# A post-norm block of windowed attention and hashed experts: a new order behind the last scores, short spare products in TensorE's waits, and narrow products in the tile loop

## The chip, the core and the metric

The kernel runs on one core of a Trainium2 chip. The core's engines run side by side and meet at semaphores: TensorE multiplies (PE in the profile, its weight loads are PEld), VectorE (DVE) and ScalarE (ACT) work on what it leaves in PSUM, GpSimd (POOL) works in SBUF and issues indirect DMAs, SyncE (SP) issues the other DMAs. The metric is the device time of one execution in microseconds, as the median of several runs.

## What is computed

The reference takes x (4 x 512 x 128, float32), adds an attention to it, normalises, adds an expert layer, and normalises again:

```python
Q, K, V = heads(x @ wq), heads(x @ wk), heads(x @ wv)           # 16 heads of 8
local = _local_window_attn(Q, K, V)                             # blocks of 32, each sees itself and the one before
GK, GV = pool(x @ wgk), pool(x @ wgv)                           # means over 8 tokens: 64 latents, 8 heads of 8
rem = softmax(mask(GQ @ GK.T / sqrt(8))) @ GV                   # causal over the latents
out = sigmoid(Q . gate_l) * local + sigmoid(Q . gate_r) * (rem @ r_out_w)
x = layernorm(x + out @ w_out)
h = mod(int(x[:, 0] + x[:, 1]), 8)                              # the token's experts: h and h + 1
y = sum over e in {h, h+1}: 0.5 * (relu(x @ W1[e] + b1[e]) @ W2[e] + b2[e])
x = layernorm(x + y)
```

## The kernel before

The 2048 tokens are 16 tiles of 128 (T = 16), four to a batch row (KT_ = 4, NB = 4). Each engine has one instruction stream, written out by hand; nothing but this order and the semaphores sets when things run.

**The tile loop** (`for t in range(T + 3)` on every engine) is a pipeline three tiles deep. In iteration t TensorE makes the scores of tile t (`score_latent`, `score_rows`), subtracts the maxima that VectorE found (`largest`, `take_off`), ScalarE takes the exponentials (`exp`), TensorE transposes them one iteration later (`turn`, line 1244), ScalarE copies them to SBUF (PTs), and TensorE multiplies with the values: `weigh(t, 0)` and `weigh(t, 1)` for the 16 windowed heads (line 1259, the transposed probabilities as weights in pieces of 32 columns), and `weigh(t, 2)` for the latent heads (line 1266, k + 1 products with all 128 columns as weights, k being the tile's place in its batch row). `normalise` (VectorE) divides by the row sums, TensorE transposes `rem` (line 1361), multiplies with r_out_w (line 1377), `gate` adds the two parts to `att`, TensorE transposes `att` (line 1340) and multiplies with w_out (line 1347), and `residual` (VectorE) adds the input, writes y and takes its moments (lines 856 to 860). GpSimd and, for the last tile, VectorE (line 1011) finish the layer norm into x1. Once per batch row `fill(("G", b))` makes the latent keys and values (lines 1148 and 1151).

**Routing.** `mark` (VectorE) finds the expert of each token of a batch row, `fill(("R", ...))` and `rank_last` count ranks with products on TensorE, `place` turns ranks into rows of a buffer `groups` in HBM, and GpSimd scatters the rows there.

**Full tiles.** Behind the 12th tile's routing some expert groups already hold full tiles of 128 tokens. `full_tiles` and `full_rows` (VectorE, lines 923 to 944) work out for FULL = 5 such tiles the expert and the first row, and write them as integers to `full_table`. SyncE reads each entry into a register (`load_table`, line 306) and issues the loads: w1f (2 x 256 KB of W1, in WR = 3 buffers, line 354) and xrow (the tokens, line 364). `columns(j)` transposes a tile on TensorE (line 1286), `up_full` makes the two up products (lines 1295 and 1299), ScalarE does the relus, `down_full` the down products (line 1310). VectorE also reads the five expert numbers into registers (line 1017), since its `full_sum` picks the bias by them; then come `moments` and `finish`.

**Other tiles.** The remaining tiles are looped over at run time (`Fori`, lines 1417 to 1436 on TensorE), 17 of them here: 16 up passes, 16 down passes and a transpose each. VectorE does half of the second relus (line 1073), copies the next columns (line 1047), and finishes the tile before (`finish`, line 1041), for which it waits until the stores before that one have landed; GpSimd issues one indirect store per tile (lines 579 and 568).

**Clock.** At the start TensorE runs products of a constant tile `spare` (line 1317) while it waits for the first data.

What stands behind the last scores (t = 16, 17, 18) is the part that the change reorders:

- VectorE, t = 16: normalise(14), full_tiles, full_rows, residual(13), full_biases, gate(14); t = 17: normalise(15), residual(14), gate(15); t = 18: residual(15). Then line 1011, mark(3), place(3), count_tiles, and the five register loads.
- TensorE, t = 16: transposes and weighing of tile 15, line 1361 (which waits for residual(13), `summed`), 1377; t = 17: lines 1340, 1347, 1361, columns(0), 1377; t = 18: up_full(0, 0), line 1340, up_full(0, 1), line 1347.
- SyncE: the five xrow loads stand ahead of w1f of the second tile, and each w1f load waits until the one before has landed.

## Time and profile before

| | us |
|---|---|
| median of 3 runs (lowest to highest) | 242.28 (241.79 to 242.59) |
| the profiled execution, its own time | 243.42 |
| its span, from the first instruction to the last | 241.4 |
| PE busy in the span | 216.1 |
| DVE, ACT, POOL busy | 151.5, 121.5, 117.3 |

The profile is of one execution. Its span leaves 2.0 us outside, and its own time lies 1.14 us above the median of the runs. "Busy" of TensorE counts pipelined products with their latency, so a high share doesn't say that the array is full. A timeline row is: start, length, engine, line, operation, output and inputs, count, and in brackets the engine's idle time before it and what ended it. PEclk and the granted clock are TensorE's clock as a share of 2.4 GHz.

### The profile page before, as it was taken

How to read it: one execution, taken by the hardware profiler on the slowest of the kernel's cores; microseconds unless marked ns; L12 is line 12 of the kernel's file. 1: busy time of each engine (PE TensorE's matmuls, PEld its weight loads, DVE VectorE, ACT ScalarE, POOL GpSimd, SP SyncE). 2: the span in 40 equal slices, each digit the busy share in tenths (PEclk: the TensorE clock that was granted, in tenths of full speed). 3: DMA queues.
4: the chain of work that ended last, by engine and by line, in shares of the span. 5: the costliest groups of instructions: out<-in, count | busy, mean ns of one | idle time of the engine just before them, and what ended most of it. 6: DMA issues, size and time to landing. Idle time of an engine off the chain costs nothing.

```text
span 241.4 us, 9967 instructions
## 1 busy us (share of the span) xinstructions
PE 216.1 (90%) x3623; PEld 182.5 (76%) x3623; DVE 151.5 (63%) x523; ACT 121.5 (50%) x360; POOL 117.3 (49%) x218
## 2 busy tenths in 40 slices
PE   7979998999999999998996899897999999999930
PEld 3545777877888678886874599886899999999920
DVE  7835457795877867888898525374556656555640
ACT  3534656665577646765754246652434353434410
POOL 6453034661744428662747330648465465545541
PEclk9988999999999999999999569999999999999995
DMA  3231130032212233120001435412112112111100
GB/s 98 57 93 45 48 91 3 3 92 90 89 33 80 72 101 92 45 69 15 27 25 44 124 110 175 133 35 66 45 49 49 54 51 55 30 38 44 34 22 7
DMA packets 18553, 14.68 MB, mean 61 GB/s; under 512 B 2646, under 2 KB 15546, under 8 KB 18512
## 3 DMA queue, kind: packets, MB, share of 16 engines
q1 hardware_dynamic: 17008, 11.83, 17.5%
q0 software_dynamic: 1216, 2.16, 2.7%
q8 instruction: 27, 0.44, 0.8%
q10 hardware_dynamic: 288, 0.13, 0.2%
q14 instruction: 14, 0.11, 0.2%
HBM read 11.43 MB, written 3.03 MB: 60 GB/s over the span
## 4 chain that ended last, share of the span: by engine, by line
PE 64%; DVE 11%; issue 9%; DMA 6%; ACT 3%; POOL 2%; DVEq 2%; POOLq 1%; ACTq 0%
PE bS L1295 9%; PE bT L1244 7%; DMA out<-yo,idx 5%; PE bV L1435 4%; PE bV L1428 4%; PE bS L1187 4%; PE bV L1259 3%; PE bS L1212 3%; PE bV L1266 3%; PE bJ L1163 3%; PE bS L1226 2%; PE bL L1347 2%; PE bT L1295 2%; PE bS L1194 2%; PE bL L1361 2%
## 5 line engine op out<-in xcount | busy, mean ns | idle before, releaser
L681 ACT ACTIVATE ha<-bS,b1c 128x128 f32<-128x128 f32 x68 | 19.4, 368 | 40.0 <-PE bS L1295 40.0
L669 ACT COPY PTs<-bT 128x512 f32<-128x512 f32 (+3 forms) x48 | 25.8, 538 | 19.4 <-PE bT L1244 19.3
L568 POOL DMA_INDIRECT out<-yo,idx x18 | 19.2, 1067 | 17.8 <-POOL idx L564 9.8
L1244 PE MATMUL bT<-ident,Pr 128*128 128x128 f32 x168 | 27.4, 282 | 0.1
L1295 PE MATMUL bS<-xsT,w_s 128*128 128x128 f32 x204 | 26.4, 279 | 0.9 <-issue 0.8
L499 POOL TENSOR_SCALAR rstd<-mv 128x1 f32<-128x1 f32 x16 | 3.8, 235 | 45.7 <-DVE mv L860 45.7
L1295 PEld LDWEIGHTS bS<-xsT,w_s 128*128 128x128 f32 x204 | 24.1, 192 | 2.1 <-issue 2.1
L1244 PEld LDWEIGHTS bT<-ident,Pr 128*128 128x128 f32 x168 | 20.5, 147 | 4.1 <-issue 3.8
L515 POOL DMA_INDIRECT groups<-x,pos x16 | 16.6, 1035 | 12.5 <-DVE pos L910 9.1
L815 DVE TENSOR_REDUCE mx<-bS 128x8 bf16<-128x512 f32 x32 | 21.4, 676 | 0.0
L656 ACT ACTIVATE Pr<-bS 128x512 f32<-128x512 f32 x32 | 19.9, 622 | 2.6 <-PE bS L1226 2.6
L1435 PE MATMUL bV<-w_s,hb 128*128 128x128 f32 x136 | 19.0, 279 | 1.4 <-DVE hb L1073 1.4
L820 DVE TENSOR_REDUCE mx<-bS 128x8 bf16<-128x128 f32 (+3 forms) x16 | 7.8, 490 | 18.0 <-issue 10.6
L1435 PEld LDWEIGHTS bV<-w_s,hb 128*128 128x128 f32 x136 | 17.0, 191 | 2.0 <-DVE hb L1073 1.8
L1428 PE MATMUL bV<-w_s,ha 128*128 128x128 f32 x136 | 18.2, 276 | 0.3 <-DVE ysum L1023 0.2
L1073 DVE TENSOR_SCALAR hb<-bT,b1c 128x128 f32<-128x128 f32 x34 | 10.4, 346 | 11.7 <-PE bT L1295 9.2
L1428 PEld LDWEIGHTS bV<-w_s,ha 128*128 128x128 f32 x136 | 16.5, 192 | 0.7 <-ACT ha L681 0.7
L1259 PE MATMUL bV<-Vx,PTs 128*32 128x18 f32 x1024 | 15.2, 186 | 1.7 <-DVE rem L836 0.8
L1259 PEld LDWEIGHTS bV<-Vx,PTs 128*32 128x32 f32 x1024 | 12.3, 111 | 4.8 <-issue 3.4
L632 ACT COPY Vx<-bJ 64x256 f32<-64x256 f32 x32 | 12.0, 374 | 7.7 <-PE bJ L1163 7.5
L1041 DVE TENSOR_SCALAR yo<-y,mv,rstd 128x128 f32<-128x128 f32 x22 | 7.6, 344 | 9.8 <-DMA out<-yo,idx 5.8
L560 POOL TENSOR_TENSOR rstd<-rstd,half 128x1 f32<-128x1 f32 x22 | 12.7, 578 | 1.7
(236 smaller groups left out, 515.5 us busy)
## 6 DMA issues: line engine op xcount, KB each, us to landing
w_s<-in_L_ffn_W SPq DMA_DIRECT2D x16, 256.0 KB
w1f<-in_L_ffn_W SPq DMA_DIRECT2D x10, 256.0 KB, 2.7
xrow<-groups SPq DMA_DIRECT2D x22, 64.5 KB, 1.8
xs<-groups SPq DMA_DIRECT2D x18, 64.0 KB
x_tok<-in_L_attn_x SPq DMA_DIRECT2D x4, 256.0 KB, 3.2
groups<-padrows SPq DMA_DIRECT2D x1, 516.0 KB, 5.7
b2r<-in_L_ffn_b SPq DMA_DIRECT2D x1, 512.0 KB, 3.7
out<-yo,idx POOLq DMA_INDIRECT x18
```

The source lines that it names most:

```text
L515: nc.gpsimd.indirect_dma_start(seg, bass.IndirectOffsetOnAxis(ap=pos[:, t:t + 1], axis=0), x1[:, t, :], None).then_inc(done, 16)
L560: nc.gpsimd.tensor_tensor(rstd2[:, s:s + 1], rstd2[:, s:s + 1], half[:, 0:1], ALU.pow).then_inc(rs_ok, 1)
L568: nc.gpsimd.indirect_dma_start(rows_out, bass.IndirectOffsetOnAxis(ap=idx[:], axis=0), yo[:, FULL - 1, :], None, bounds_check=T * P - 1, o ...
L656: nc.scalar.activation(Pr[:, t % 2, j, :].rearrange("p (z c) -> p z c", z=2), own[j], ACT.Exp, scale=SCALE).then_inc(exped[j], 1)
L669: nc.scalar.copy(PTs[:, j, 0:m, :], bT[:, 0:m * P].rearrange("p (c q) -> p c q", c=m)).then_inc(turned_out, 1)
L681: nc.scalar.activation(dst[:, c, :], src[:, c * P:(c + 1) * P], ACT.Relu, bias=bias_of(c)).then_inc(relu, 1)
L815: nc.vector.tensor_reduce(mx[:, j, :].rearrange("p (z h) -> p z h", z=2), own[j].rearrange("p z (h k) -> p z h k", h=4), AX.X, ALU.max).th ...
L1244: last = nc.tensor.transpose(bT[:, c * P:(c + 1) * P], Pr[:, t % 2, j, c * P:(c + 1) * P], ident[:])
L1259: last = mm(bV[i * W:(i + 1) * W, a * PW:(a + 1) * PW], PTs[:, j, c, i * W:(i + 1) * W], Vx[:, q, i, a, :], start=True, stop=True)
L1295: last = mm(bank_of(c)[:, c * P:(c + 1) * P], w[:, c * P:(c + 1) * P], xsT[:], start=True, stop=True)
L1428: mm(bY[:, 0:D], ha[:, c, :], w2_s[:, e, c, :], start=(c == 0), stop=False)
L1435: last = mm(bY[:, 0:D], hb[:, c, :], w2_s[:, a, c, :], start=False, stop=(c == FC - 1))
```

## The change

1. **VectorE behind the last scores.** residual(13) is moved ahead of full_tiles and full_rows, gate(14) ahead of full_biases. The table work loses instructions: `m` comes from one instruction with a constant `tile_scale` (made by GpSimd at the start), `taken` goes behind mark(3), and the two casts into `full_table` become one. The five register loads are split: two behind residual(14), two ahead of residual(15), one behind mark(3).
2. **TensorE behind the last scores.** 42 products of `spare` (bfloat16, 128 x 256) into bJ in ten places; columns(0) goes from t = 17 to t = 18, ahead of up_full(0, 0); rank_last goes from between up_full(2, 0) and down_full(1, 1) to directly behind up_full(1, 1).
3. **SyncE.** w1f of tiles 1 and 2 goes between the xrow loads, and the loads no longer wait for each other (a semaphore for each of the three buffers).
4. **Tile loop.** The latent weighing and the latent keys and values are cut into pieces of 32 weight columns: (k + 1) products of 128 columns become 4 (k + 1) of 32; of `fill(("G", b))` 1 and 4 products become 2 and 16. ScalarE scales 64 rows of the keys in place of 128.

The core of the diff:

```diff
             def load_full_weights(j):
-                if j >= 1:
-                    sp.wait_ge(w1f_in, 32 * j)
                 if j >= WR:
                     sp.wait_ge(up_b, j - WR + 1)
...
                 sp.dma_start(xrow[:, j * XW:(j + 1) * XW], seg[bass.ds(rows[j], P), :]).then_inc(full_in[j], 16)
-            for j in range(1, FULL):
+                if 1 <= j + 1 < WR:
+                    experts += load_table(sp, full_table[:, 0, :], [j + 1], full_ok, E - 1)
+                    load_full_weights(j + 1)
+            for j in range(WR, FULL):
                 experts += load_table(sp, full_table[:, 0, :], [j], full_ok, E - 1)
-                if j < WR:
-                    load_full_weights(j)
-            for j in range(WR, FULL):
                 load_full_weights(j)
...
-                link(nc.vector.tensor_copy(full_table[:, 0, :], expert_of[0:1, :]))
-                nc.vector.tensor_copy(full_table[:, 1, :], rowf[0:1, :]).then_inc(full_ok, 1)
...
+                nc.vector.tensor_copy(full_table[:], found[0:1, :, :]).then_inc(full_ok, 1)
...
+                if t == T + 2:
+                    experts += load_table(dve, full_table[:, 0, :], [2, 3], full_ok, E - 1)
+                if t >= 3:
+                    residual(t - 3)
                 if t == T:
                     upto = full_tiles()
                     full_rows(upto)
-                if t < T:
-                    largest(t, 2)
-                    largest(t, 0)
-                if t >= 3:
-                    residual(t - 3)
+                if t == T + 1:
+                    experts = load_table(dve, full_table[:, 0, :], [0, 1], full_ok, E - 1)
...
+                if 2 <= t < T + 2:
+                    gate(t - 2)
                 if t == T:
                     full_biases()
-                if 2 <= t < T + 2:
-                    gate(t - 2)
...
             mark(NB - 1)
+            take_tiles(upto)
+            experts += load_table(dve, full_table[:, 0, :], [4], full_ok, E - 1)
             place(NB - 1)
             count_tiles()
-
-            experts = load_table(dve, full_table[:, 0, :], range(FULL), full_ok, E - 1)
...
-                    mm(dst[:, 0:NL], wgk_s[:], xp[:, q, :], start=True, stop=True)
+                    for i in range(LD // W):
+                        mm(dst[i * W:(i + 1) * W, 0:NL], wgk_s[:, i * W:(i + 1) * W], xp[:, q, :], start=True, stop=True)
 
                     for m in range(KT_):
-                        last = mm(dst[:, NL + m * LD:NL + (m + 1) * LD],
-                           xph[:, m, :, :].rearrange("p h l -> p (h l)"), wgv_s[:], start=True, stop=True)
+                        for i in range(BLK):
+                            last = mm(dst[i * W:(i + 1) * W, NL + m * LD:NL + (m + 1) * LD],
+                                      xph[:, m, :, :].rearrange("p h l -> p (h l)")[:, i * W:(i + 1) * W], wgv_s[:],
+                                      start=True, stop=True)
...
                     for c in range(k + 1):
-                        last = mm(bV[:, HP * PW:(HP + LP) * PW], PTs[:, j, c, :],
-                                  GVx[:, b % 2, c, :, :].rearrange("p a w -> p (a w)"), start=(c == 0), stop=(c == k))
+                        for i in range(BLK):
+                            last = mm(bV[i * W:(i + 1) * W, HP * PW:(HP + LP) * PW], PTs[:, j, c, i * W:(i + 1) * W],
+                                      GVx[:, b % 2, c, :, :].rearrange("p a w -> p (a w)"), start=(c == 0),
+                                      stop=(c == k), skip_group_check=True)
...
+            def keep_busy(n):
+                for _ in range(n):
+                    mm(bJ[:, 0:256], spare[:, 0:P], spare[:, 0:256], start=True, stop=True)
...
                 if t == T + 2:
+                    keep_busy(6)
+                    columns(0)
+                    keep_busy(4)
                     up_full(0, 0)
...
+                if t > T:
+                    keep_busy(6 if t == T + 1 else 2)
...
-                if j == 1:
-                    rank_last()
...
+                if j == 0:
+                    rank_last()
```

**VectorE, t = 16 and 17.** Before, from the table work to the normalisation of tile 15 (`rs`); `y`, `st`, `mv` are residual(13), `chosen`, `b1p`, `b1x` are full_biases, `att` is gate(14):

```order
L944 CAST full_table<-rowf 1x5 [waits dve_step]
L856 TENSOR_TENSOR y<-bL,x_tok 128x128 [waits ln_done,proj_up]
L859 BN_STATS st<-y 128x6 [waits summed]
L860 BN_AGGR mv<-st 128x2 [waits dve_step]
L949 TENSOR_TENSOR chosen<-expert_of,efl 128x40 [waits b1d_ok]
L951 TENSOR_TENSOR b1p<-b1d,chosen 128x320 [waits dve_step]
L954 TENSOR_REDUCE b1x<-b1p 128x40 [waits dve_step]
L846 TENSOR_TENSOR att<-bL,gat 128x128 [waits attT_up,rem_up]
L849 TENSOR_TENSOR att<-att,loc 128x128 [waits dve_step]
L829 RECIPROCAL rs<-bV 128x24 [waits gates_ok,pv_done]
```

The changed kernel, from residual(14) in t = 17 to residual(15) in t = 18:

```order
L859 BN_AGGR mv<-st 128x2 [waits dve_step]
L306 TENSOR_LOAD full_table [waits full_ok]
L306 ISA x2
L306 TENSOR_LOAD full_table
L306 ISA x2
L845 TENSOR_TENSOR att<-bL,gat 128x128 [waits attT_up,rem_up]
L848 TENSOR_TENSOR att<-att,loc 128x128 [waits dve_step]
L306 TENSOR_LOAD full_table [waits full_ok]
L306 ISA x2
L306 TENSOR_LOAD full_table
L306 ISA x2
L855 TENSOR_TENSOR y<-bL,x_tok 128x128 [waits ln_done,proj_up]
```

The residual left its place behind the table and stands ahead of it; four register loads stand around gate(15), where before nothing stood.

**TensorE, t = 17 and 18.** Before, from the last latent weighing to up_full(0, 0):

```order
L1266 MATMUL bV<-GVx,PTs 128x72 x3
L1340 MATMUL bL<-ident,att 128x128 [waits gated]
L1347 MATMUL bL<-wout_s,attT 128x128 [waits attT_out]
L1361 MATMUL bL<-ident,rem 128x128 [waits summed,normed]
L1286 MATMUL bS<-ident,xrow 128x128 [waits full_in0]
L1377 MATMUL bL<-rout_s,remT 128x128 [waits remT_out]
L1295 MATMUL bS<-xsT,w1f 128x128 [waits xT_out,w1f_in]
```

In the changed kernel (line 1281 is keep_busy):

```order
L1274 MATMUL bV<-GVx,PTs 32x72 x15
L1281 MATMUL bJ<-spare 128x256 x6
L1358 MATMUL bL<-ident,att 128x128 [waits gated]
L1281 MATMUL bJ<-spare 128x256 x4
L1367 MATMUL bL<-wout_s,attT 128x128 [waits attT_out]
L1281 MATMUL bJ<-spare 128x256 x6
L1385 MATMUL bL<-ident,rem 128x128 [waits summed,normed]
L1281 MATMUL bJ<-spare 128x256 x4
L1401 MATMUL bL<-rout_s,remT 128x128 [waits remT_out]
L1281 MATMUL bJ<-spare 128x256 x6
L1299 MATMUL bS<-ident,xrow 128x128 [waits full_in0]
L1281 MATMUL bJ<-spare 128x256 x4
```

The spare products fill each wait for another engine, and the transpose of the first full tile moved behind line 1377's product.

## Rows read from the trace of the kernel before

**Rows 1.** The page: busy time and share of TensorE, its granted clock in tenths

```profile
PE 216.1 (90%) x3623; PEld 182.5 (76%) x3623; DVE 151.5 (63%) x523; ACT 121.5 (50%) x360; POOL 117.3 (49%) x218
PEclk9988999999999999999999569999999999999995
```

**Rows 2.** Busy time by stretch: PE, PEld, DVE, ACT, POOL, granted clock, DMA

```profile
130.00:140.00 10.00, 6.94 (x57) 5.60 (x58) 5.96 (x26) 1.83 (x6) 4.76 (x8) 0.62 0.36 101
```

**Rows 3.** The timeline, TensorE's weight loads in the tile loop

```profile
91.87 0.97 PEld L1151 LDWEIGHTS bJ<-wgv_s,xph 128*128 128x128 f32 x8
...
102.85 0.35 PEld L1259 LDWEIGHTS bV<-Vx,PTs 128*32 128x32 f32 x32 [0.17 <-issue]
...
103.09 0.55 PEld L1163 LDWEIGHTS bJ<-wvg,xT 128*32 128x32 f32 x32
...
105.54 0.97 PEld L1266 LDWEIGHTS bV<-GVx,PTs 128*128 128x128 f32 x8 [0.19 <-ACT PTs L669]
```

**Rows 4.** The chain that ended last, tile loop: start, length, engine, line

```profile
40.06 0.78 PE bV L1266 x6
...
91.10 0.44 PE bS L1226 x4
...
92.09 0.89 PE bJ L1151 x8
...
113.14 0.28 PE bV L1266 x2
```

**Rows 5.** The timeline, VectorE in t = 16: table work, then residual(13)

```profile
128.46 0.16 DVE L925 TENSOR_TENSOR full<-nextrow,efl 128x8 f32<-128x8 f32 x1
...
131.86 0.29 DVE L856 TENSOR_TENSOR y<-bL,x_tok 128x128 f32<-128x128 f32 x1
```

**Rows 6.** The timeline, TensorE in t = 16 to 18

```profile
132.29 0.40 PE L1361 MATMUL bL<-ident,rem 128*128 128x128 f32 x1 [1.56 <-DVE y L856]
...
134.22 1.98 PE L1266 MATMUL bV<-GVx,PTs 128*128 128x72 f32 x8 [0.25 <-ACT PTs L669]
...
139.44 1.92 PE L1295 MATMUL bS<-xsT,w1f 128*128 128x128 f32 x8
```

**Rows 7.** The timeline from residual(15) to place(3)

```profile
143.27 0.29 DVE L856 TENSOR_TENSOR y<-bL,x_tok 128x128 f32<-128x128 f32 x1 [2.97 <-PE bL L1347]
...
146.94 0.14 PEld L1286 LDWEIGHTS bS<-ident,xrow 128*128 128x128 f32 x1
...
147.55 0.19 DVE L886 TENSOR_TENSOR onehot<-near,efl 128x32 bf16<-128x32 f32 x1
...
149.33 0.19 DVE L905 TENSOR_TENSOR cand<-bJ,nextrow 128x32 f32<-128x32 f32 x1 [1.59 <-PE bJ L1277]
```

**Rows 8.** The timeline: DMA issues behind the table, TensorE waiting for weights

```profile
133.72 0.96 SPq L354 DMA_DIRECT2D w1f<-in_L_ffn_W  x2
...
134.87 3.72 SPq L364 DMA_DIRECT2D xrow<-groups  x4
...
152.74 0.97 PEld L1295 LDWEIGHTS bS<-xsT,w1f 128*128 128x128 f32 x8 [0.82 <-DMA w1f<-in_L_ffn_W]
```

**Rows 9.** The timeline, VectorE's first full tile behind the register loads

```profile
156.87 0.29 DVE L1023 TENSOR_TENSOR ysum<-fsum,b2s 128x128 f32<-128x128 f32 x1 [3.87 <-issue]
```

**Rows 10.** The timeline, first tiles of the run-time loop

```profile
162.38 1.50 PE L1295 MATMUL bS<-xsT,w_s 128*128 128x128 f32 x12
...
167.38 0.75 PE L1435 MATMUL bV<-w_s,hb 128*128 128x128 f32 x4 [1.23 <-DVE hb L1073]
...
168.16 1.60 PE L1295 MATMUL bS<-xsT,w_s 128*128 128x128 f32 x12
...
169.75 0.36 DVE L1041 TENSOR_SCALAR yo<-y,mv,rstd 128x128 f32<-128x128 f32 x1 [1.97 <-DMA out<-yo,xrow]
...
172.81 1.60 PE L1295 MATMUL bS<-xsT,w_s 128*128 128x128 f32 x12
...
176.59 1.50 PE L1295 MATMUL bS<-xsT,w_s 128*128 128x128 f32 x12
```

41 lines of the change are left out of this document (26 added, 15 removed).

## The prediction

> **What bounds the kernel now.** I read the page first: TensorE is busy for 90% of the span, and its granted clock is full nearly everywhere except at the start, at the end and in two slices two thirds of the way through [rows 1]. The table by stretch puts a number on that dip: 0.62 on average between 130 and 140 us, with TensorE busy for only 6.94 of 10 us [rows 2]. That is just behind the last scores, the part that the change reorders. Next I read the chain that ended last. In the tile loop it runs mostly along TensorE, in the order of its instructions, with the latent weighing and the latent keys and values as links [rows 4]. From tile 12 on it alternates with VectorE. Behind the last scores it goes through VectorE and TensorE in turn, and two more delays follow: 3.87 us in which VectorE only loads registers before its first full tile [rows 9], and the first two tiles of the run-time loop, which come slower than the later ones [rows 10]. So three places can pay: the loop, the stretch from 128 to 153 us, and the hand-over to the run-time loop. A fourth, the pace of that loop, isn't touched.
>
> **The tile loop (part 4 of the change).** An fp32 product is two passes. A pass with 128 weight columns costs 0.97 / 8 = 0.12 us in a group, and 0.11 us in the chain (0.89 for 8) [rows 3, 4]. The new form isn't in the trace with these tiles, but both its neighbours are: 32 passes of 32 columns take 0.35 us where 18 columns move (0.011 us a pass) and 0.55 us where 64 to 96 move (0.017 us) [rows 3]. The new ones move 72 and 64 columns, so I take the nearer row, 0.0175 us. A latent weighing of one product then falls from 0.222 to 8 x 0.0175 = 0.140 us. The chain holds eight such weighings, the first and the last of them in [rows 4], with 44 passes or 22 products together: 22 x 0.082 = 1.8 us. The latent keys and values cost 2 + 8 passes = 1.1 us each time, and become 4 + 32 passes = 0.65 us, four times on the chain: 1.7 us. Together 3.5 us. Behind TensorE stand VectorE and ScalarE with a few tenths of slack in some iterations, so I enter **3.0 us**. The bounds are 0 (a narrow pass costs a quarter of a wide one, so four of them save nothing) and 5.5 us (0.011 us a pass, all of it on the chain).
>
> The rows show that four narrow weight loads cost far less than one wide one: 4 x 0.017 = 0.07 against 0.12 us [rows 3]. The Trainium skill says otherwise (TensorE: Matmul & The Clock Gate, section "LDWEIGHTS (loading the stationary operand)"): a load takes its columns divided by 1.2 ns, whatever the rows, so 27 ns for 32 columns, and four would cost what one of 128 does. By that the loop gains nothing, and the forecast would be 3.0 us later. The 32 loads in 0.55 us, 17 ns each, speak against it.
>
> **VectorE behind the last scores (part 1).** The table work took from 128.46 to the start of the residual at 131.86, 17 instructions in 3.4 us, 0.2 us each [rows 5]. Three instructions go, so it needs 2.8 us; but the residual's three (0.3 us each, by the row of y) now stand ahead. So the table is ready about 0.3 us later than the old place of the residual suggests, near 132.8 us, 0.7 us later than before. What this delays is the SyncE chain: first weights issued at 133.72, first token tile at 134.87 [rows 8]; both 0.7 us later. What it buys: TensorE's transpose at 132.29, which waited 1.56 us for that residual [rows 6], can go at 131.2. Tile 15's latent weighing (1.98 us at half clock [rows 6]) then costs 0.6 us and ends near 133.3, where before it ended at 136.2. From 132.8 on VectorE has no wait left: gate(14), biases, normalise(15) and residual(14) are 12 instructions of about 0.3 us, to 136.6. Then come two register loads. Five took 3.87 us [rows 9], the first of a batch more than the rest, so two are about 1.7 us, to 138.3; gate(15) follows, and two more loads, to 140.5. TensorE meanwhile: transpose, copy and product behind residual(14) end near 137.1.
>
> **TensorE's spare products (part 2)** cost 0.11 us each, by the four of 256 columns in 0.44 us [rows 4]; 42 of them are 4.6 us. Thirty lie in t = 16 and 17, in waits for VectorE, which runs through. The last twelve (1.3 us) lie in a row with columns(0): 6 spare (0.65), columns(0) (0.3), 4 spare (0.45, beside the 0.3 us copy of its result), up_full(0, 0) (0.9), register loads and 2 spare (0.3), transpose (0.3), up_full(0, 1) (0.9), w_out (0.35): 4.1 us from 137.1, so residual(15) starts at 141.25 in place of 143.27 [rows 7], **2.0 us** earlier. The token tile lands at about 137.5 to 138.2, so most of the first six are waited out anyway. The up products cost 0.9 us for 8 passes since the clock stays up; at half clock 8 took 1.92 us [rows 6] where 12 take 1.50 at full clock [rows 10]. If this cover is gone, the twelve cost their 1.3 us.
>
> From residual(15) to the end of mark(3) it is 143.27 to 147.74 [rows 7], nothing of which changes: 145.7 now. **rank_last's new place** turns a free slot into a wait. TensorE reaches it behind up_full(1, 1), whose end at 146.94 [rows 7] moves to about 145.0; the marks come at 145.7. With its own 0.25 us rank_last ends at 145.95, where before TensorE stood at 146.94 and had rank_last still ahead (0.2). Gain of TensorE here: 1.2 us. Queued behind the wait are all its down products, and 0.7 us of the 2.0 are lost.
>
> **Weights (part 3).** TensorE waited 0.82 us for the fourth tile's weights [rows 8], issued late since each load waited for the one before. Now they go as soon as the first buffer is free (about 141 us) and are there long before. The wait goes: 0.8 us. TensorE reaches the run-time loop 1.2 + 0.8 = **2.0 us** early.
>
> **Hand-over.** VectorE's first full tile started at 156.87. Of that go 3.87 us of loads [rows 9], 2.0 us by the earlier marks, and 1.59 us of waiting for ranks [rows 7]; take_tiles and one load come in (1.25 us): about 150.7, 6 us earlier. Then VectorE is no longer behind in the full tiles; its last head store goes out about 3 us (without part 4) earlier. Before, the second half of the first tile's relus came 1.23 us late, and the next finish waited 1.97 us for the stores [rows 10]. The first tiles started at 162.38, 168.16, 172.81, 176.59 [rows 10]: 5.78, 4.65 and 3.78 us apart. With the third distance as the pace the first two shrink by 2.0 and 0.9 us: **2.8 us**. What is late next is the chain of stores (one tile's store must land before the next), whose pace is close to TensorE's, so I expect nothing from later tiles. GpSimd's extra instruction at the start lies beside ScalarE and TensorE; I cost it at nothing, at most 0.2 us.
>
> **The sum.** Against the profiled span: 241.4 - 3.0 - 2.0 - 2.8 = 233.6. With the 2.0 us outside it is 235.6, and the profiled execution lay 1.14 us above the median: **234.5 us**.
>
> **The rivals.**
> - *The narrow products save nothing* (a quarter of the price for a quarter of the columns, or the loop is held by VectorE and ScalarE). For it: VectorE is in the chain from tile 12 on. Against: the narrow rows of the same shape. 234.5 + 3.0 = 237.5. Chance 0.15.
> - *The clock falls all the same* behind the last scores, or in a loop whose products got shorter. For it: it fell where TensorE was busy for 6.94 of 10 us [rows 2], and narrow products leave more waits. Then the two ups, the transposes and the last twelve spares take up to twice as long, 1.5 to 3 us on the path to residual(15): 237.0. Chance 0.12.
> - *The register loads and the late table end up on the path*: gate(15) waits for two loads, the tiles for a table 0.7 us later, and a longer wait at rank_last eats more than 0.7 us. The 2.0 us of TensorE fall to about 0.8: 235.7. Chance 0.10.
> - *Narrow products that run one behind another* end slower. On the chain are 22 x 8 + 4 x 36 = 320 narrow passes, which replace 9.1 us. The other gains are 4.8 us. Slower than before from (9.1 + 4.8) / 320 = 0.043 us a pass. At half the price of a wide one, 0.055 us, it is 17.6 us: 234.5 + 3.0 + 8.5 = 246.0. For it: these accumulate over c into the same columns, which lines 1259 and 1163 don't. Against: line 1194 adds to what line 1187 left in pieces of 32 and shows no such price. Chance 0.05.
> - That the change does more than I enter (5.5 in the loop) gives 232.0: chance 0.05.
>
> **How the numbers follow.** The forecast itself, 234.5 with 233.0 to 236.2, has 0.53. The range reaches up over the first three rivals to 238.2 and down to 231.8, and leaves out the fourth. Within 0.3% (about what a measurement of this kernel can tell from no change) is 241.6 to 243.0. Faster 0.93, same 0.02, slower 0.05.
>
> **What the changed profile would show.** The clock of 130 to 140 us at 1.0; the latent weighing with 32 passes in about 0.6 us; full_table 0.7 us behind its old place on an unshifted scale; VectorE without a wait from the table to residual(14); TensorE waiting about 0.7 us at rank_last; no wait for w1f; VectorE's first full tile 6 us earlier plus the loop's gain; the first three distances of the run-time loop near 3.8 us. Wrong it would be if tile 12 doesn't start earlier by 2 to 3 us, or if the run-time loop starts less than 4 us earlier in all.

## The result, and the profile after

The changed kernel takes 239.28 us (median of 20 runs, 237.60 to 242.81), the kernel before 243.32 (20 runs beside them, 241.79 to 244.66): ratio 0.984, 95% interval 0.981 to 0.986, so 1.6% or 4.0 us faster. Forecast were 234.5 us and a range up to 238.2. The direction was right; the gain was about half of what was forecast, and the time lies above the range. Some executions of this kernel run at a lower granted clock and over 1.5% longer: every ratio here leaves them out, every median has them in.

The profiled execution has a span of 236.5 us, 4.9 less than before. The page (busy time, granted clock by slices, the instruction queue) and one row of the table by stretch (busy time of PE, PEld, DVE, ACT, POOL, granted clock, DMA):

```profile
PE 212.2 (90%) x4009; PEld 176.2 (75%) x4009; DVE 147.3 (62%) x521; ACT 120.6 (51%) x360; POOL 117.8 (50%) x219
PEclk9999999999999999999999999999999999999995
q8 instruction: 30, 0.49, 0.9%
...
130.00:140.00 10.00, 8.43 (x93) 6.52 (x92) 4.30 (x18) 1.93 (x7) 3.83 (x7) 1.00 0.54 158
```

The dip of [rows 1, 2] is gone, 1.00 in place of 0.62, and so is the one at the start. The line on queue 8, the instruction queue, has a partner on the page of before that I hadn't looked at (packets, MB, share):

```profile
q8 instruction: 27, 0.44, 0.8%
```

TensorE behind the last scores, as the timeline of the changed kernel shows it (start, length, engine, line, idle time before and what ended it):

```profile
127.07 0.29 DVE L855 TENSOR_TENSOR y<-bL,x_tok 128x128 f32<-128x128 f32 x1 [0.38 <-PE bL L1367]
...
130.56 0.16 DVE L944 CAST full_table<-found 1x10 int32<-1x10 f32 x1
130.64 0.71 PE L1274 MATMUL bV<-GVx,PTs 128*32 128x72 f32 x32
...
136.38 0.33 PE L1299 MATMUL bS<-ident,xrow 128*128 128x128 f32 x1 [0.92 <-DMA xrow<-groups]
...
138.91 0.39 PE L1281 MATMUL bJ<-spare 128*128 128x256 bf16 x2 [0.62 <-issue]
...
140.57 0.29 DVE L855 TENSOR_TENSOR y<-bL,x_tok 128x128 f32<-128x128 f32 x1 [4.43 <-PE bL L1367]
...
145.11 0.19 PE L1288 MATMUL bJ<-onehot,before 128*128 128x32 bf16 x1 [0.90 <-DVE onehot L885]
...
149.87 0.32 DVE L1027 TENSOR_TENSOR ysum<-fsum,b2s 128x128 f32<-128x128 f32 x1 [0.33 <-DVE tile_table L970]
```

residual(13) starts at 127.07 and the last latent weighing takes 0.71 us (1.98 in [rows 6]). From there the gain shrinks: TensorE waits 0.92 us for the first token tile, 0.62 where its own two register loads stand, and 0.90 at rank_last. residual(15) starts at 140.57 (143.27 in [rows 7]). No up product waits for weights any more ([rows 8]: 0.82), and VectorE's first full tile starts 7.0 us earlier than in [rows 9]. The first tiles of the run-time loop (lines 1308 and 1045 are the up products and the finish of [rows 10]):

```profile
159.53 1.50 PE L1308 MATMUL bS<-xsT,w_s 128*128 128x128 f32 x12
...
163.22 1.60 PE L1308 MATMUL bS<-xsT,w_s 128*128 128x128 f32 x12
...
164.81 0.36 DVE L1045 TENSOR_SCALAR yo<-y,mv,rstd 128x128 f32<-128x128 f32 x1 [1.94 <-DMA out<-yo,xrow]
...
167.88 1.60 PE L1308 MATMUL bS<-xsT,w_s 128*128 128x128 f32 x12
...
171.66 1.50 PE L1308 MATMUL bS<-xsT,w_s 128*128 128x128 f32 x12
```

They are 3.69, 4.66 and 3.78 us apart. The first distance has shrunk (5.78 before), the second not (4.65): the finish still waits 1.94 us for stores.

### The profile page after: what moved, and what is told of

It is laid out like the page before. It is cut to its first block, busy times and chain, and to the rows that moved or that the text cites. A ratio compares the mean times of both kernels' runs of the same rounds, so it can differ in the third digit from the quotient of the medians.

```text
span 236.5 us, 10737 instructions
## 1 busy us (share of the span) xinstructions
PE 212.2 (90%) x4009; PEld 176.2 (75%) x4009; DVE 147.3 (62%) x521; ACT 120.6 (51%) x360; POOL 117.8 (50%) x219
## 3 DMA queue, kind: packets, MB, share of 16 engines
q1 hardware_dynamic: 17008, 11.83, 17.9%
## 4 chain that ended last, share of the span: by engine, by line
PE 74%; DVE 6%; issue 5%; DMA 4%; POOL 3%; ACT 3%; SPq 1%; POOLq 0%; ACTq 0%; DVEq 0%
PE bS L1308 12%; PE bT L1251 7%; PE bV L1452 6%; PE bV L1459 5%; PE bS L1194 4%; PE bV L1266 4%; PE bS L1219 4%; PE bJ L1170 3%; PE bV L1323 3%; PE bT L1308 3%; PE bS L1233 2%; PE bL L1367 2%; PE bS L1201 2%; PE bV L1274 2%; DMA out<-yo,idx 2%
## 5 line engine op out<-in xcount | busy, mean ns | idle before, releaser
L680 ACT ACTIVATE ha<-bS,b1c 128x128 f32<-128x128 f32 x68 | 19.4, 368 | 38.0 <-PE bS L1308 38.0
L567 POOL DMA_INDIRECT out<-yo,idx x18 | 19.4, 1076 | 17.5 <-POOL idx L563 9.6
L1251 PEld LDWEIGHTS bT<-ident,Pr 128*128 128x128 f32 x168 | 19.5, 141 | 5.4 <-issue 4.1
L514 POOL DMA_INDIRECT groups<-x,pos x16 | 16.5, 1034 | 11.7 <-DVE pos L909 8.4
L655 ACT ACTIVATE Pr<-bS 128x512 f32<-128x512 f32 x32 | 20.1, 629 | 3.0 <-PE bS L1233 3.0
L1459 PE MATMUL bV<-w_s,hb 128*128 128x128 f32 x136 | 18.5, 277 | 0.0
L1077 DVE TENSOR_SCALAR hb<-bT,b1c 128x128 f32<-128x128 f32 x34 | 10.5, 347 | 11.7 <-PE bT L1308 11.0
L504 POOL TENSOR_SCALAR x<-y,mv,rstd 128x128 f32<-128x128 f32 x15 | 13.0, 867 | 1.6
L559 POOL TENSOR_TENSOR rstd<-rstd,half 128x1 f32<-128x1 f32 x22 | 12.5, 567 | 1.7
```

The source lines that it names most:

```text
L504: nc.gpsimd.tensor_scalar(x1[:, t, 0:D], y[:, q, :], mv[:, q, 0:1], rstd[:, q, :], ALU.subtract, ALU.mult).then_inc(ln_done, 1)
L514: nc.gpsimd.indirect_dma_start(seg, bass.IndirectOffsetOnAxis(ap=pos[:, t:t + 1], axis=0), x1[:, t, :], None).then_inc(done, 16)
L567: nc.gpsimd.indirect_dma_start(rows_out, bass.IndirectOffsetOnAxis(ap=idx[:], axis=0), yo[:, FULL - 1, :], None, bounds_check=T * P - 1, o ...
L655: nc.scalar.activation(Pr[:, t % 2, j, :].rearrange("p (z c) -> p z c", z=2), own[j], ACT.Exp, scale=SCALE).then_inc(exped[j], 1)
L680: nc.scalar.activation(dst[:, c, :], src[:, c * P:(c + 1) * P], ACT.Relu, bias=bias_of(c)).then_inc(relu, 1)
L1251: last = nc.tensor.transpose(bT[:, c * P:(c + 1) * P], Pr[:, t % 2, j, c * P:(c + 1) * P], ident[:])
```

## The experiments

18 runs were made: e1 to e4 on one chip, e5 to e8, e17 and e18 on a second, e9 to e12 on a third, e13 to e16 on a fourth. The kernel before took 243 us on some chips and 249 us on others, so ratios are to the before of the same chip. All stretches of the table are from the profiled executions, one each. That one lay above the median of its kernel by 3.3 us in e9, 2.5 in e5 and 1.7 in e18, under it by 2.3 in e15, and within 1.9 us of it elsewhere. The stretches are: the start of the scores' first maximum of tile 15 (line 819, 820 before), from there to residual(15) (`y`), to the transpose of the first run-time tile, to that of the third, and to the end of the span. "Packet pauses" is the sum of the pauses of TensorE's weight loads (PEld) of 0.35 us and more between 20 and 125 us that have no releaser and end 1.2 to 1.7 us behind a packet of the instruction queue, and the longest.

| kernel (before, median) | ratio, 95% interval | tile 15 | to y | to first | to third | to end | packet pauses |
|---|---|---|---|---|---|---|---|
| before (243.3) | 1 | 123.1 | 20.1 | 17.6 | 10.6 | 70.0 | 0.8, 0.8 |
| changed | 0.984 (0.981-0.986) | 121.3 | 19.3 | 17.4 | 8.5 | 70.0 | 2.4, 0.8 |
| e1 (249.0) | 0.999 (0.994-1.003) | 125.0 | 21.0 | 22.1 | 9.7 | 70.1 | 3.1, 0.9 |
| e2 | 0.998 (0.995-1.002) | 126.4 | 22.2 | 19.5 | 8.5 | 71.0 | 2.8, 0.8 |
| e3 | 0.998 (0.993-1.003) | 124.7 | 22.9 | 22.6 | 9.4 | 69.5 | 2.7, 0.8 |
| e4 | 0.990 (0.985-0.995) | 124.1 | 22.4 | 19.7 | 9.1 | 68.8 | 2.1, 0.6 |
| e5 changed (243.1) | 0.981 (0.976-0.986) | 124.3 | 19.6 | 17.4 | 8.5 | 69.9 | 4.4, 1.8 |
| e6 | 0.977 (0.973-0.981) | 123.8 | 18.7 | 16.3 | 8.6 | 69.7 | 4.9, 2.1 |
| e7 | 0.981 (0.975-0.988) | 124.3 | 19.3 | 17.9 | 8.6 | 70.2 | 3.6, 2.1 |
| e8 | 0.981 (0.975-0.987) | 123.8 | 19.0 | 17.4 | 8.6 | 69.7 | 5.7, 2.1 |
| e9 before (248.7) | 0.996 (0.993-1.000) | 127.1 | 21.9 | 20.5 | 9.2 | 70.0 | 2.8, 0.7 |
| e10 changed | 0.996 (0.992-1.001) | 125.0 | 22.2 | 19.2 | 9.2 | 69.0 | 1.8, 0.5 |
| e11 | 0.994 (0.990-0.998) | 125.9 | 23.4 | 19.5 | 9.1 | 69.2 | 3.5, 0.7 |
| e12 | 1.010 (1.003-1.017) | 126.9 | 22.8 | 19.5 | 9.1 | 69.3 | 2.3, 1.1 |
| e13 changed (249.4) | 0.994 (0.990-0.999) | 125.3 | 22.9 | 19.4 | 8.5 | 69.5 | 3.9, 1.3 |
| e14 | 1.001 (0.997-1.005) | 126.1 | 23.7 | 19.4 | 9.1 | 68.9 | 2.4, 0.8 |
| e15 | 1.015 (1.008-1.023) | 128.2 | 22.8 | 19.5 | 9.1 | 70.1 | 7.4, 1.7 |
| e16 | 0.988 (0.981-0.996) | 123.8 | 22.8 | 19.3 | 8.5 | 71.0 | 2.4, 0.7 |
| e17 (242.9) | 0.994 (0.990-0.997) | 125.6 | 19.0 | 17.5 | 8.6 | 69.7 | 3.8, 2.1 |
| e18 | 0.981 (0.976-0.986) | 124.1 | 20.3 | 16.3 | 8.6 | 70.3 | 4.6, 2.3 |

### One part alone, one part undone

**e1: the kernel before with part 4 of the change alone.** The same three edits as in the diff of part 4, nothing else.

> The kernel before with part 4 alone (narrow latent weighing, narrow latent keys and values). Theory A, the narrow products are shorter but the time goes into waits behind them (ScalarE's copy behind the keys and values, pauses of TensorE's instruction stream, VectorE in the later tiles): 0 to 0.7 us faster than before, ratio 0.997 to 1.000. Theory B, they are worth the 3.0 us entered in the prediction and the missing gain is behind the last scores: 3 us faster, ratio 0.988.

Ratio 0.999, with an interval that leaves out B's 0.988: no difference that could be measured, by A.

**e2: the changed kernel with wide products**; its diff is part 4 undone.

> The changed kernel with the wide latent products of before (part 4 undone, parts 1 to 3 kept). Theory A: about as fast as the changed kernel, 0 to 1 us slower than it, ratio to before 0.984 to 0.988, and less spread from run to run, since the loop's products keep their length. Theory B: 3 us slower than the changed kernel, ratio 0.996.

Ratio 0.998 with an interval that holds B's 0.996 and leaves out A's 0.984 to 0.988. But both were set against the changed kernel's 0.984, and that kernel itself didn't run on this chip, so this decides nothing, and e11 repeats it.

**e3: without the spare products** behind the last scores.

```diff
-                for _ in range(n):
+                for _ in range(0):
                     mm(bJ[:, 0:256], spare[:, 0:P], spare[:, 0:256], start=True, stop=True)
```

> The changed kernel without its 42 spare products, all else kept. If the clock behind the last scores is what they buy: granted clock of 128 to 140 us falls to about 0.6 as before, and the run is 1 to 2.5 us slower than the changed kernel (ratio 0.988 to 0.994). If the residual's new place alone fills the waits enough: clock stays at 1.0 and the run is 0.5 to 1.3 us faster than the changed kernel, since twelve spare products lay in a row with the first full tile (ratio 0.979 to 0.982).

The granted clock between 125 and 150 us is 0.73, where the changed kernel has 0.93 on such a chip (e13) and 1.00 on the faster ones:

```profile
125.00:150.00 25.00, 19.55 (x304) 16.29 (x302) 13.25 (x56) 9.65 (x30) 9.61 (x15) 0.73 0.29 89
```

From residual(15) to the first run-time tile it takes 22.6 us; the changed kernel took 19.2 and 19.4 on such chips, and e1, which has no spare products there either, 22.1 at 0.80. The spare products keep this clock up, and by these traces they are worth 3 us. By the ratios it is less: 0.998 against the 0.994 and 0.996 of the changed kernel on such chips, 0.5 to 1 us, which the intervals don't tell from nothing.

**e4: VectorE's five register loads back behind count_tiles.**

> The changed kernel with VectorE's five register loads back behind the tile counts, in one batch. By the prediction VectorE's first full tile then starts 2.6 us later and the first two distances of the run-time loop grow again to about 5 and 4.5 us: 1.5 to 2.5 us slower than the changed kernel (ratio 0.990 to 0.994). Rival: the run-time loop's first tiles were late for another reason (the chain of stores), and the run is within 0.5 us of the changed kernel.

Ratio 0.990, and 119.9 us from tile 15 to the end against 119.6 and 120.2 (e10, e13, on other chips). VectorE's first full tile starts 12.5 us behind residual(15), where the changed kernel has 9.3 in each of three traces, and yet the first to the third run-time tile take 9.1 us against 9.2 and 8.5. Where these loads stand is worth nothing that shows.

**e5: the changed kernel again, and e6 to e8 beside it.**

> The changed kernel itself, beside the kernel before on this chip, as the measure for the other runs of this batch. Theory A (the gain doesn't hang on the chip): ratio 0.981 to 0.986, as measured first. Theory B (part of the first gain was the state of the executions, since the same parts taken away singly gave ratios of 0.990 to 0.999 on another chip): 0.985 to 0.993. The trace should again show no stretch at half clock between 126 and 140 us, the first tile of the run-time loop 4 to 7 us earlier than before, and latent weighings of 32 passes in 0.6 to 0.7 us.

0.981, by A. The clock is 1.00 from 125 to 150 us, as expected. The first run-time tile is not 4 to 7 us earlier than before: its transpose starts at 161.3 us, where the first trace of before has 160.8, in an execution 2.5 us above its median.

**e6: rank_last in its place of before.**

```diff
+                if j == 1:
+                    rank_last()
                 if j == 3:
                     more_tiles([2, 3])
                 down_full(j, 1)
...
-                if j == 0:
-                    rank_last()
```

> The changed kernel with the ranks of the last batch row back in the place of before, ahead of the second down product of the second full tile. Theory A (at the early place TensorE waits 0.9 us for the marks, and all down products are queued behind that wait): TensorE gains 0.5 to 0.9 us to its run-time loop; since VectorE's place(3) then waits for the ranks, its first full tile starts 1 to 2 us later, but VectorE catches up: 0 to 0.9 us faster than the changed kernel, ratio to it 0.996 to 1.000. Theory B (the early place is what lets VectorE be in time for the stores): 1 to 2.5 us slower than the changed kernel, and the second distance of the run-time loop grows by 1 us or more.

237.67 us against 238.96, ratio 0.977 against 0.981, with intervals that overlap. The trace has the wait of 0.90 us gone, and from residual(15) to the first run-time tile 16.3 us against 17.4; the distance behind it doesn't grow (8.6 against 8.5). That is A: by the trace the early place costs 1.1 us and buys nothing. e17 and e18 on the same chip have the same pair, 17.5 with the early place and 16.3 with the late one; on a slower chip it isn't there (19.4 in e13, 19.4 in e14).

**e7: SyncE's order and waits of before.**

> The changed kernel with SyncE's order of before (each load of w1f waits for the one before, all token tiles ahead of the second tile's weights). Theory A: the wait for weights comes back at the third or fourth full tile with 0.8 us or more, since TensorE arrives earlier than before: 0.8 to 1.8 us slower than the changed kernel. Theory B (the store chain behind the first run-time tiles hides it): the wait is in the trace, but the second distance of the run-time loop (4.66 us) shrinks by as much, and the time differs from the changed kernel by less than 0.5 us.

The wait for weights is back, at the second full tile:

```profile
145.98 0.97 PEld L1307 LDWEIGHTS bS<-xsT,w1f 128*128 128x128 f32 x8 [1.67 <-DMA w1f<-in_L_ffn_W]
```

To the first run-time tile it takes only 0.5 us longer, since the marks are there by the time TensorE comes to rank_last, and its 0.90 us of waiting is gone. The distance to the third tile doesn't shrink as B has it (8.6). The median is 2.2 us higher (241.20), but its six runs spread from 237.2 to 244.3 and the ratio is the same: the wait is shown, a loss of time by it is not.

**e8: the first token tile issued ahead of the first weights.**

```diff
                 if j == 0:
-                    experts += load_table(sp, full_table[:, 0, :], [j], full_ok, E - 1)
-                    load_full_weights(j)
                     sp.wait_ge(scattered, 16 * EARLY)
                 sp.dma_start(xrow[:, j * XW:(j + 1) * XW], seg[bass.ds(rows[j], P), :]).then_inc(full_in[j], 16)
+                if j == 0:
+                    experts += load_table(sp, full_table[:, 0, :], [j], full_ok, E - 1)
+                    load_full_weights(j)
```

> The changed kernel with the first token tile issued ahead of the first tile's weights. In the changed kernel TensorE waits 0.9 to 1.2 us for that token tile. Theory A (this wait is on the path): the token tile is issued 0.5 to 1.0 us earlier, the wait shrinks by that, and the run is 0.4 to 1.0 us faster than the changed kernel. Theory B: the weights, 0.25 MB each and now issued later, land later than TensorE needs them, or VectorE's register loads set the transpose behind it anyway: within 0.4 us of the changed kernel or slower.

239.47 us against 238.96, with the same ratio: no gain. B's first half: the wait for `xrow` is gone, and a line later stands one of the same size for the weights:

```profile
139.50 0.97 PEld L1309 LDWEIGHTS bS<-xsT,w1f 128*128 128x128 f32 x8 [1.24 <-DMA w1f<-in_L_ffn_W]
```

**e16: without the twelve spare products of t = 18.**

> The changed kernel without the twelve spare products of t = 18, which stand in a row with the first full tile (the thirty of t = 16 and 17 stay). Theory A (they lie on the path behind the register loads, 0.11 us each, where the token tile has landed): 0.5 to 1.3 us faster, if the clock stays at 1.0. Theory B (the first six lie in the wait for the token tile, and without them the clock falls in the two up products): 0 to 1.5 us slower, with a stretch at half clock behind 138 us.

247.11 us against 247.18 (e13), ratio 0.988 against 0.994: same or slightly faster. The stretch from tile 15 to residual(15) didn't shrink (22.8 and 22.9), and the clock of 125 to 150 us fell from 0.93 to 0.86. The twelve cost nothing that shows, and neither theory is told from the other.

### The loop: narrow products, and what TensorE's pauses are

**e9 and e10: before and changed, e11 (wide again) and e12 (weighing narrow, keys and values wide) on the same chip.**

> The kernel before itself, for a trace from the same chip as the next three. Ratio 1.00. Theory: the larger pauses in TensorE's stream for which the profile has no releaser (0.3 to 2 us) end 1.3 to 1.6 us behind the end of a 16 KB packet of the instruction queue, in this trace as in the others; here 27 packets, and 1.5 to 3 us of such pauses between 20 and 125 us.

> The changed kernel itself, beside the next two. Ratio to before 0.980 to 0.988; 30 instruction packets, and 2.5 to 5 us of pauses behind them between 20 and 125 us, more than in the kernel before, since the narrow products bring 772 more instructions into a loop that has become shorter.

> The changed kernel with wide products in the loop, now with the changed kernel on the same chip. Theory A (the narrow products save 3 us, as forecast): 2.5 to 3.5 us slower than the changed kernel. Theory B (a good part of their saving is lost to instruction pauses and to ScalarE and VectorE): 0.5 to 2 us slower. Theory C (they save nothing): within 0.4 us.

> The changed kernel with narrow products in the latent weighing alone; latent keys and values wide. In the changed kernel TensorE waits 0.4 us longer for ScalarE's copy of the latent values once they are computed sooner. Theory A: the keys and values' share is 1.7 us, as forecast, so 1.3 to 1.7 us slower than the changed kernel. Theory B: ScalarE takes over behind them, within 0.6 us of the changed kernel. Instruction packets 29 in place of 30.

Medians 247.38, 247.58, 247.92 and 250.95. e9 is the kernel before against itself and comes out at 0.996, so 0.4% is what such a comparison leaves open. The ratio of 0.980 to 0.988 that I expected of e10 was a miss. On this chip neither the change nor its part 4 makes a difference in the medians (e11: theory C), and half of part 4 alone makes the kernel 1.0% slower than before, which no theory had. The profiled execution of e12 was its fastest (249.26). In e9 2.8 us of pauses end behind packets, as expected; in e10 only 1.8 us, under the 2.5 that I expected and under e9's. More narrow products didn't bring more pauses here.

What pauses are these? In e10 as in every trace, the larger ones inside a group of products carry no releaser. This is e5 at tile 12: 27 of the 32 passes of line 1170 run, then TensorE stands for 1.67 us (PE; 1.83 PEld), and behind it ScalarE (2.33 us) and VectorE (2.54):

```profile
101.08 0.43 SPq L346 DMA_DIRECT2D w_s<-in_L_ffn_W  x1
...
103.00 0.53 PEld L1170 LDWEIGHTS bJ<-wvg,xT 128*32 128x32 f32 x27
...
105.36 0.28 PE L1170 MATMUL bJ<-wvg,xT 128*32 128x64 f32 x3 [1.67 <-issue]
105.36 0.12 PEld L1170 LDWEIGHTS bJ<-wvg,xT 128*32 128x32 f32 x3 [1.83 <-issue]
```

The DMA view of the same trace, from 103.05 to 104.10 us, has one packet of queue 8 (the instruction queue), beside the last of the 0.5 MB of expert weights (`w_s`) that SyncE issued at 100.7 and 101.1:

```profile
q1 hardware_dynamic: 295, 0.14, 46.4%
q0 software_dynamic: 30, 0.06, 15.3%
q8 instruction: 1, 0.02, 5.5%
```

It starts at 103.11 and ends at 104.03, and the one before it started at 97.21. In the first trace of the changed kernel the packet of this place started at 98.80, ahead of the weights (issued at 99.24), and line 1170 ran its 32 passes in one piece. I read the pause as TensorE out of instructions. In all twenty traces together, weight loads stand 31 times for 0.70 us or more without a releaser between 20 and 125 us, and every one of these pauses ends 1.2 to 1.6 us behind the end of a packet. The numbers fit: 772 more instructions (386 passes and their loads) made three more packets of 16 KB, about 64 bytes each. The Trainium skill (Vector Engine (DVE) Microarchitecture Reference, section "Instruction fetch and dispatch (NX sequencer)") gives the same width, exactly 64 bytes, for an instruction of VectorE; for TensorE the packets here agree with it.

**e15 moves the packets' boundaries by half a packet, e17 by a whole one**, e13 and e14 stand beside e15.

```diff
-            for _ in range(7):
+            for _ in range(5):
                 mm(bL[:], spare[:, 0:P], spare[:], start=True, stop=True)
+            for _ in range(64):
+                mm(bL[0:W, 0:16], spare[:, 0:W], spare[:, 0:16], start=True, stop=True)
```

(e17: 2 in place of 5, 133 in place of 64.)

> The changed kernel itself, beside the next three. Ratio 0.980 to 0.986 on a chip whose kernel before takes 243 us, 0.992 to 1.000 on one where it takes 248 to 249 us.

> The changed kernel with two of the seven first spare products (512 columns) taken out and 64 tiny ones (32 weight columns, 16 moving) put in, 62 products or 124 instructions more ahead of all others: nothing of the work changes, but the boundaries of TensorE's 16 KB instruction packets (some 256 instructions each) fall half a packet earlier in the program. Theory A (the larger pauses are waits for instruction packets): they move to other lines, each still 1.3 to 1.6 us behind a packet's end, and their sum between 20 and 125 us changes by 0.3 us or more in either direction; the time follows it, within 1.5 us of the changed kernel. Theory B (they belong to the instructions at which they stand): same lines, same time within 0.4 us.

> The changed kernel with five of the seven first spare products taken out and 133 tiny ones put in: 128 products, 256 instructions more ahead of all others. By the packets counted so far (772 instructions more made three more packets of 16 KB, so 64 bytes an instruction) that is one whole packet, so the boundaries fall where they fall in the changed kernel. Theory A (where the boundaries fall is what cost the half shift its 6.4 us): the larger pauses are back near the places of the changed kernel, packets 31, and the ratio to before is that of the changed kernel on such a chip (0.98 to 0.986 on one at 243 us, 0.992 to 1.000 on one at 248 us), plus at most 1 us for the tiny products' 3.7 us at the start. Theory B (the tiny products themselves, or a larger number of instructions, cost the time): slower than before by 2% or more, as the half shift or worse.

e15 takes 253.62 us, 6.4 more than e13, for the same work: the first maxima of tile 0 come only 0.3 us later. That is far outside the 1.5 us of A and the 0.4 of B. The pauses moved to other lines, always behind a packet, as A has it. Their sum rose from 3.9 to 7.4 us, and three are over 1.5 us, as here:

```profile
55.51 0.44 SPq L346 DMA_DIRECT2D w_s<-in_L_ffn_W  x1
...
61.17 0.14 PEld L1387 LDWEIGHTS bL<-ident,rem 128*128 128x128 f32 x1 [1.56 <-issue]
```

The packet ahead of it started at 58.78. From 56.0 to 58.7 the DMA view shows nothing but the weights that were issued at 55.1 and 55.5:

```profile
q1 hardware_dynamic: 672, 0.52, 62.1%
```

The whole shift (e17) brings the boundaries back, to the very pass:

```profile
102.93 0.53 PEld L1170 LDWEIGHTS bJ<-wvg,xT 128*32 128x32 f32 x27
...
105.57 0.12 PEld L1170 LDWEIGHTS bJ<-wvg,xT 128*32 128x32 f32 x3 [2.10 <-issue]
```

27 passes and then a pause, as in e5. Its packet pauses sum to 3.8 us in four pieces, e5's to 4.4 in five. It is slower than the changed kernel all the same (ratio 0.994 against 0.981), which I hadn't expected above 1 us: the 133 tiny products delay tile 0's first maxima by 2.8 us against e5. By tile 12 the two are level, but e5 had lost 1.7 us to a dip of the clock at the start, so at least that much of the delay stays. e15 has nothing of this delay and yet the largest loss. By its marks e17 is neither: A allowed a ratio of 0.990 at most, B had 1.02 or more. A's places came, and the 3 us that it lacks are about the delay at the start. So the place of the boundaries moves the pauses, and a larger number of instructions alone doesn't cost what e15 lost; but e15 ran on a slower chip than e17, and a whole shift wasn't run there. Of e15's 6.4 us the two profiled spans show 4.1 (249.6 and 245.5), 3.5 of it in packet pauses; the rest I can't place.

**e14 and e18: single changes put together**, rank_last late with the token tile first, and rank_last late without the last twelve spares.

> The changed kernel with the ranks of the last batch row in their place of before and the first token tile issued ahead of the first weights. Theory A (both moves were on the path: 1.3 us by the medians for the ranks, up to 0.5 us for the token tile): 1.0 to 2.0 us faster than the changed kernel, the best so far. Theory B (what TensorE gains behind residual(15) is given back at the stores of the first run-time tiles): within 0.5 us of the changed kernel.

> The changed kernel without the twelve spare products of t = 18 and with the ranks of the last batch row in their place of before, the two single changes that came out best by their medians. Theory A (both were on the path): ratio to before 0.972 to 0.980 on a chip at 243 us, 0.983 to 0.990 on one at 248 us. Theory B (the one gives back what the other gains): within 0.3% of the changed kernel.

e14 takes 248.02 against 247.18 (e13), e18 239.55 with ratio 0.981, as the changed kernel on such chips. Neither does what A said: e18 is B's, e14 is 0.8 us behind e13, just outside B's 0.5. In e18 the gain of e6 is there between residual(15) and the run-time loop (16.3 us), but residual(15) itself comes 20.3 us behind tile 15 where e5 has 19.6 and e6 18.7: the clock falls once more (up_full(0, 0) takes 1.47 us, 1.13 in the changed kernel). So in this execution, in which TensorE waits 1.69 us for the token tile, the last twelve spares would have been cover. The best kernel that ran is e6, by its median; its interval overlaps that of the changed kernel.

## Why the prediction was wrong

The reference itself moved: the median of the kernel before was 243.32 beside these runs, not 242.28, and the profiled execution, which I took as 1.14 us above the median, lay 0.1 above it; the changed kernel's lay 1.05 below. That is 2.2 of the 4.8 us of the miss, and luck of the profiled executions, not mechanism. The rest is in the span: 4.9 us less, not 7.8 (of the 2.9 us, 0.3 comes back outside it, 1.7 us in place of 2.0).

- **The loop, forecast 3.0, was the step that failed most: narrow products were priced by their own groups, without what they do to the wide products beside them.** Tile 15 starts only 1.85 us earlier, and 1.72 of that is there by tile 1: before's profiled execution had TensorE at half clock for 3.4 us around 18 us (granted clock 0.91 in 0 to 20 us, 1.00 after). That isn't the change's doing: seven of the twenty traces have it, with wide and with narrow products. So the loop gave 0.1 us in this pair, and the other 1.7 are luck. The narrow groups themselves came near the forecast: 32 passes follow one another in 0.64 us and 24 in 0.51, 0.020 to 0.021 us a pass where 0.0175 was forecast, and keys and values take 0.57 us where the wide ones took 1.06. But here is a weighing of three products (6 wide passes, 24 narrow ones) with what stands ahead of it and behind it, before and after:

```profile
99.32 0.38 PE L1377 MATMUL bL<-rout_s,remT 128*128 128x128 f32 x2
99.54 0.79 PE L1266 MATMUL bV<-GVx,PTs 128*128 128x72 f32 x6
100.17 0.60 PE L1244 MATMUL bT<-ident,Pr 128*128 128x128 f32 x4
100.60 0.39 PE L1212 MATMUL bS<-GKx,GQT 128*128 128x128 f32 x2
...
97.52 0.39 PE L1401 MATMUL bL<-rout_s,remT 128*128 128x128 f32 x2
97.84 0.58 PE L1274 MATMUL bV<-GVx,PTs 128*32 128x72 f32 x24
98.35 0.66 PE L1251 MATMUL bT<-ident,Pr 128*128 128x128 f32 x4
98.87 0.46 PE L1219 MATMUL bS<-GKx,GQT 128*128 128x128 f32 x2
```

From start to start the three groups took 0.22, 0.63 and 0.43 us, 1.28 together, and now take 0.32, 0.51 and 0.52, 1.35 together: the weighing is shorter by 0.12, the two wide groups beside it are longer by 0.19. Added up over TensorE's rows from tile 1's first maximum to tile 15's (start to start, idle time left out), the latent weighings fell from 7.9 to 6.9 us and the keys and values from 3.2 to 1.7, but line 1377's product rose from 3.6 to 4.3 and the transposes of line 1244 from 17.9 to 18.5. TensorE's time without idle fell from 98.8 to 98.0 us, by 0.8; on the chip of e9 to e12 it is 100.4 and 100.2 with wide products and 99.1 with narrow ones. In e12, with the weighing alone narrow, it is 101.2, so that half saves nothing, and the gain is that of the keys and values. Why the neighbours get longer no run shows.

- **The stream of instructions**, which I had treated as keeping up, is the second thing that the loop's term lacked. In the first pair 1.6 us went into packet pauses (0.8 before, 2.4 after), and some into ScalarE, for whose copy of the latent values TensorE waits 0.70 us where it was 0.27. On the chip of e9 to e12 it is the other way round: fewer packet pauses in e10 than in e9 and e11, and tile 1 to tile 15 in 104.8 us where they take 106.6 and 107.0, although the medians differ by 0.3 us at most. So one pair of traces doesn't price part 4: it is worth between nothing and 2 us in traces, nothing measurable in e1 and e11, and 3 us are excluded by e1's interval. The rival "the narrow products save nothing" was right in its result; of its mechanisms the one on the price comes near, but not by the narrow loads: 32 of them take 0.53 us, 17 ns each. The Trainium skill (TensorE: Matmul & The Clock Gate, section "LDWEIGHTS (loading the stationary operand)") has columns / 1.2 ns, 27 ns for 32 columns; these rows don't agree.
- **Behind the last scores, forecast 2.0 to residual(15)**, the trace gives 0.85 (20.1 to 19.3). The order did what was expected of it (no wait of VectorE from the table to residual(14), the clock at 1.00, the weighing at 0.71). The late table came as forecast too: its cast starts 9.3 us behind tile 15's first maximum, where the last one of before started 8.7 us behind it, and the first token tile is issued 12.6 us behind it in place of 11.7. What I priced at nothing or too low took the gain back: the wait for the token tile (0.92; I had it waited out by the first six spares) and 0.62 us where TensorE's own two register loads stand, which I had at 0.3 with two spares.
- **rank_last**, forecast to take back 0.7 of that gain: the wait is 0.90 us, and e6 prices it at 1.1 on its chip. The weights' wait of 0.8 is gone as forecast, and e7 brings it back. Together they gained 0.2 us net where I had 0 (the 2.0 was to be held to the run-time loop).
- **Hand-over, forecast 2.8: 2.1.** The first distance shrank as expected (5.78 to 3.69), the second stayed (4.65 to 4.66). The second distance, forecast to shrink by 0.9, is the part that failed: VectorE's first full tile came 5.2 us earlier without the loop's shift, but its fourth waits 2.42 us for ScalarE's sum, the second and third are finished behind it, and the finish in the run-time loop waits 1.94 us for their stores as before (1.97). e4 goes further: with VectorE's first full tile 3.2 us later the first to the third run-time tile take 9.1 us, between e13's 8.5 and e10's 9.2, so the early start that I built this term on isn't shown to pay.
- **The clock** behind the last scores stayed up in the first result; that rival fell there. On the slower chips it is 0.93 from 125 to 150 us in the changed kernel, and 0.73 without the spares (e3), as in e9. **Register loads and late table**: e4 shows no cost of VectorE's loads in either place. But the rest of this rival came near: it had the 2.0 us fall to 0.8 with the tiles waiting for a later table and a longer wait at rank_last, and residual(15) gained 0.85, with TensorE waiting for the token tile.

By the marks set in advance: the run-time loop's first tile starts 2.9 us earlier in all, under the 4 that I had named as the limit, and tile 12 starts 1.8 us earlier, under 2 to 3. Both said "wrong", and rightly.

**What stays open.** The gain hangs on the chip: 1.6 and 1.9% in two comparisons whose before is at 243 us, 0.4% [-0.1, 0.8] and 0.6% [0.1, 1.0] on two chips at 249 us. There the stretch from tile 15 to residual(15) gained nothing (22.2 and 22.9 us, e9 21.9). In all twelve traces from the slower chips VectorE stands for 2.3 to 2.4 us and ScalarE for 2.9 to 3.0 beside GpSimd's scatters of tile 14, in none of the eight others. Before, at tile 14 on the first chip, the two maxima follow the scatter without a wait:

```profile
115.33 1.08 POOL L515 DMA_INDIRECT groups<-x,pos  x1 [1.66 <-DVE pos L910]
...
116.13 0.56 DVE L820 TENSOR_REDUCE mx<-bS 128x8 bf16<-128x384 f32 x1
```

and the same instructions of the same kernel in e9:

```profile
116.94 1.08 POOL L515 DMA_INDIRECT groups<-x,pos  x1 [1.67 <-DVE pos L910]
...
118.33 0.96 POOL L515 DMA_INDIRECT groups<-x,pos  x1 [0.30 <-issue]
...
119.94 0.56 DVE L820 TENSOR_REDUCE mx<-bS 128x8 bf16<-128x384 f32 x1 [2.33 <-issue]
120.03 0.58 ACT L669 COPY PTs<-bT 128x512 f32<-128x512 f32 x1 [3.02 <-PE bT L1244]
```

No trace tells what holds them. Why e12 was the slowest on its chip, by 3 us, is open. Nor was it tried whether moving SyncE's expert loads away from the packets takes the long pauses out; that packets come late behind these loads is read from where they stand in e5, e15 and the first trace, and not from a run in which the loads were moved. Against it as the whole cause stands a pause of 1.14 us in e12 (at 44.4 us), whose packet had no other DMA beside it.

## What to carry to other kernels

Price a new form of product together with the groups ahead of it and behind it, from start to start, and not by its own group. Count the instructions of the engine that bounds, as well as their time: here an unrolled stream came in packets, and a change that makes products more numerous moves every boundary behind it. Before you believe a difference of 1 or 2% between two orders of such a kernel, shift the stream by a fraction of a packet with idle instructions at the start: if that alone moves the time by as much, the comparison says little about the edit. And look at the profile's own median and at short dips of the clock in the reference execution before you charge them to the change.

## What the runs showed of the hardware

- TensorE's weight loads stood for 0.70 us or more with no releaser in the tile loop 31 times in twenty traces, each time until 1.2 to 1.6 us behind the end of a 16 KB packet of the instruction queue. The longest was 2.3 us (e18). A packet holds about 256 instructions (772 more made three more); between 20 and 125 us one comes every 4.4 to 5.3 us on average.
- The same work with the boundaries half a packet elsewhere took 2.6% longer (253.62 against 247.18).
- All nine pauses of 1.5 us and more stand behind a packet that started 2.2 to 3.6 us behind the issue of 0.5 MB of loads; but packets behind such loads also made pauses of only 0.7 to 0.9 us. That the loads are the cause is not shown.
- A group of passes of 32 weight columns between groups of 128 columns makes its neighbours longer: the fp32 product ahead takes 0.31 us where it was 0.22, four transposes behind it 0.49 to 0.52 where they were 0.44.
- 32 fp32 passes of 32 weight columns and 72 moving take 0.53 us of loads and 0.71 us in all (0.64 to the next group's start), also where they accumulate.
- Tiny bf16 products (32 weight columns, 16 moving) cost 28 ns each: 3.72 us for 133 in a row.
